# A fused state-space and expert kernel: TensorE signals the end of each matmul group by a drain

## The reference, cut to what matters

```python
x = x + _layernorm(_L0_attn_ref(_layernorm(x), ...))      # four state-space layers
x = x + _layernorm(_L0_ffn_ref(_layernorm(x), w1, w2, router_w))

# inside _L0_ffn_ref: x is 8192 tokens of 128 channels, 8 experts, 2 per token
probs = softmax(x @ router_w.T)
topk_weights, selected_experts = top_k(probs, 2)
for e in range(8):
    ew = sum(topk_weights * (selected_experts == e), axis=-1, keepdims=True)
    h = x @ w1[e].T                          # 128 -> 512
    y = (h[:, 256:] * silu(h[:, :256])) @ w2[e].T        # 256 -> 128
    out = out + y * ew
```

## Time and profile before

| what | value |
|---|---|
| median of 2 runs | 1078.75 us (1078.02 to 1079.48) |
| the profiled execution, its own time | 1082.16 us |
| its span (first to last instruction) | 1080.4 us |
| TensorE matmuls busy | 750.3 us, 69% of the span |
| VectorE busy | 779.1 us, 72% |
| ScalarE busy | 553.7 us, 51% |
| GpSimd busy | 478.7 us, 44% |

### The profile page before, as it was taken

One profiled execution on the slowest core, in us unless ns is written; L12 is line 12 of the kernel. 1 busy time (PEld: TensorE's weight loads), 2 busy tenths in 40 slices (PEclk: granted clock), 3 DMA queues, 4 the chain that ended last, 5 costly groups with the idle time before them and its releaser, 6 DMA issues.

```text
span 1080.4 us, 25428 instructions
## 1 busy us (share of the span) xinstructions
PE 750.3 (69%) x8885; PEld 637.1 (59%) x8886; DVE 779.1 (72%) x1919; ACT 553.7 (51%) x1130; POOL 478.7 (44%) x672
## 2 busy tenths in 40 slices
PE   0039357694878947695878876585878999999800
PEld 0028257573876747574876655464767877788700
DVE  8977876588575966588675998634455655699987
ACT  7627941179103951079103887434445656556545
POOL 2113323256442654257342776645566645655300
PEclk9999779898998979898888985578999999999955
DMA  7606699972999269981995002222334443211002
GB/s 283 268 1 205 192 386 386 344 258 92 355 353 374 93 231 387 341 308 43 363 387 239 1 11 78 76 81 91 116 122 134 138 132 116 77 35 35 23 39 117
DMA packets 114369, 197.50 MB, mean 183 GB/s; under 512 B 17372, under 2 KB 38376, under 8 KB 113512
## 3 DMA queue, kind: packets, MB, share of 16 engines
q1 hardware_dynamic: 107624, 182.62, 47.8%
q0 software_dynamic: 6656, 13.64, 4.0%
HBM read 164.38 MB, written 31.85 MB: 182 GB/s over the span
## 4 chain that ended last, share of the span: by engine, by line
PE 28%; issue 26%; POOL 18%; DVE 14%; ACT 7%; another core or an unknown queue 4%; DMA 2%; POOLq 1%; SPq 0%; ACTq 0%; DVEq 0%
PE bank L1212 12%; POOL zbuf L635 6%; PE bank L1230 6%; POOL rstd_of L624 5%; PE bank L1062 3%; PE bank L1040 2%; POOL z_sorted L695 1%; POOL sums L615 1%; DMA toep<-kernels_dram 1%; DVE stats L1852 1%; PE bank L1184 1%; POOL mean_of L620 1%; POOL m L622 1%; ACT ln_tmp L910 1%
## 5 line engine op out<-in xcount | busy, mean ns | idle before, releaser
L1062 PE MATMUL bank<-zbuf,toep 128*128 128x128 f16 (+3 forms) x3328 | 141.3, 203 | 95.5 <-DVE zbuf L1440 72.1
L1062 PEld LDWEIGHTS bank<-zbuf,toep 128*128 128x128 f16 x3328 | 137.9, 100 | 99.5 <-issue 48.6
L1212 PE MATMUL bank<-toep 128*128 128x256 f16 x1452 | 174.9, 276 | 11.3 <-issue 6.9
L1797 DVE TENSOR_TENSOR glu_work<-bank,glu_work 128x512 f32<-128x512 f32 x121 | 80.7, 689 | 118.9 <-issue 63.0
L1212 PEld LDWEIGHTS bank<-toep 128*128 (+1 forms) x1452 | 139.3, 99 | 35.4 <-issue 17.6
L635 POOL TENSOR_TENSOR zbuf<-zbuf,w_cur 128x256 f32<-128x256 f32 x120 | 90.0, 752 | 142.0 <-DVE zbuf L1504 142.0
L958 ACT ACTIVATE glu_work<-bank 128x512 f32<-128x512 f32 x121 | 68.9, 596 | 142.2 <-PE bank L1212 85.7
L695 POOL DMA_INDIRECT z_sorted<-toep x104 | 105.8, 1017 | 75.7 <-PE bank L1212 25.5
L1504 DVE TENSOR_REDUCE zbuf<-bank 128x256 f32<-128x512 f32 x128 | 87.1, 687 | 70.5 <-PE bank L1062 70.5
L1097 PE MATMUL bank<-wo_cur,glu_work 128*128 128x256 f32 x512 | 134.8, 408 | 2.5 <-ACT glu_work L855 2.2
L855 ACT ACTIVATE glu_work<-bank,unscale_cur 128x512 f32<-128x512 f32 x64 | 42.7, 668 | 165.0 <-PE bank L1084 164.7
(11 more groups left out here) (268 smaller groups left out, 1478.3 us busy)
## 6 DMA issues: line engine op xcount, KB each, us to landing
toep<-kernels_dram SPq DMA_DIRECT2D x104, 1024.0 KB, 13.9
glu_work<-kernels_dram SPq DMA_DIRECT2D x16, 1024.0 KB, 14.0
toep<-z_sorted SPq DMA_DIRECT2D x73, 128.0 KB
y_sorted<-toep SPq DMA_DIRECT2D x73, 128.0 KB
toep_last<-kernels_dram SPq DMA_DIRECT2D x8, 1024.0 KB, 14.1
z_sorted<-ln_tmp SPq DMA_DIRECT2D x2, 3584.0 KB, 26.2
hres<-in_x SPq DMA_DIRECT2D x1, 4096.0 KB, 12.9
toep<-in_x SPq DMA_DIRECT2D x1, 4096.0 KB, 21.8
```

The source lines that it names most:

```text
L1062: last = MM(dst[:, d * (B // 4):, :], toep_slot(g)[:, c, d * P:(d + 1) * P, k], z_conv[:, 0:QUADS - d * (B // 4), g * GROUP + c].rearrange ...
L1212: last = MM(out[:, piece % 2 * XP:(piece % 2 + 1) * XP], w1_row[:, pw, weights_at(s, piece * P, P)], xT_s[:, px * XP:(px + 1) * XP], start ...
L1797: TT(inner[:, s.at % 2, :], bank[3 + s.at % 2 * 2][:, :], gate_act[:, s.at % 2, :], ALU.mult).then_inc(s_inner, 1)
```

## The change

In the three helpers of the expert loop the increment no longer rides on the last matmul of the group. A drain instruction of TensorE is put behind the group, and the drain carries the increment. What is computed, the order of all else, all waits and all other engines' code are as before. There is one drain for each group, 315 in an execution.

```diff
@@ transpose_in
-                last.then_inc(s_xT, 1)
+                pe.drain().then_inc(s_xT, 1)
@@ first_product
-                last.then_inc(s_hid, 1)
+                pe.drain().then_inc(s_hid, 1)
@@ second_product
-                last.then_inc(s_yps, 1)
+                pe.drain().then_inc(s_yps, 1)
```

## The result

The changed kernel takes 1255.44 us (1251.55 to 1259.33) against 1078.75 us, a ratio of 1.1645 with an interval of 1.160 to 1.169. The forecast was 1275 us. The profiled span is 1257.6 us against 1080.4. All but 1 us of that lies in the expert loop: from its first matmul to the end of its last the loop takes 502.5 us instead of 326.3, which is 176.2 us more.

What follows compares the result with a forecast made beforehand. TensorE was taken to bound the dense and nearly the later sorted steps. To 1078.75 us came 124 us of drain costs (1203) and 72 us of drains held by GpSimd's bursts, giving 1275 us, range 1165 to 1390.

Steps and rivals of the forecast that it cites:

- The bound and the direction: Expert loop: TensorE bounds dense and nearly later sorted steps; slower by more than 22 us at 0.95.
- The rival on the other side: Locked cycles: drains signal past late completions, silu comes 2 to 3 us earlier, at most 18 us gained; same or faster 0.05.
- The price in dense steps: Dense cycles: each drain adds 0.33 us, from emptying the queue, the drain itself and restarting.
- Emptying: Behind each group: 0.16 us of the last matmul, formerly overlapped by the next group, is laid bare.
- The drain's own 0.05: Behind each group: the drain waits for the matmuls before it and itself adds about 0.05 us.
- The restart's 0.12: After each drain: restarting costs 0.12 us, taken from a dense cycle that waits at its start, 1.46 against 1.34 us.
- The price in sorted steps: Sorted cycles: drains, bare register instructions, slow starts and register loads add 3.4 us per cycle, bounds 2.0 and 4.5.
- The hold: Beside GpSimd's indirect DMA bursts: drains wait for late completions until the flush, 72 us more; 1275 us in all, chance 0.35.
- The sign named for the hold: Drains of over 1 us beside GpSimd's issues would show it; at most 0.3 us throughout would refute it.
- the matmuls in flight: Named way to be wrong: the delay beside bursts goes with the number of matmuls in flight; no size given.
- The clock: Rival, sorted cycles: TensorE falls to 1.2 GHz, 53 us on top for a third of them, 1328 us; chance 0.28.
- the 1203 forecast for drains that aren't held: Rival, expert loop: drains escape the wait beside GpSimd's bursts, so the sum of 1203 us stands; chance 0.25.

Runs made afterwards that it cites:

- the bare drains: Against the changed kernel, increments back on each group's last matmul, a drain without increment behind: 1202.78 us (ratio 1.1585) on one chip, 1264.58 us (1.1703) on another.

## Why the prediction was right, and which terms weren't

**The bound and the direction** hold: TensorE's stream was the bound, and no other engine covered the gaps. The rival on the other side, a signal that gets past the late completions, did not come: drains are held too.

**The price in dense steps**, 0.33 us a drain, was 0.245 us. Emptying was right at 0.16 us. The drain's own 0.05 was 0.02 us. The restart's 0.12 was 0.06 us; the row it was taken from the earlier trace rows held a passed wait besides. Behind the first product it is 0.33 us over the former distance, where such a wait does follow.

**The price in sorted steps**, 3.4 us a cycle, was about right. The single distances over the former ones add up to 0.245 (between transposes), 0.62 (to the second product), 0.46 and 0.49 (behind its halves, without a hold), 0.48 (between the wide ones) and 0.6 (to the transposes, the turns included), 2.9 us; the slow start of the two narrow groups, 0.78 us instead of 0.61 from first to last start, adds 0.3 us where I had 0.5.

**The hold** was the mis-sized term: 72 us forecast. Against the bare drains on the chip without it, the distances behind narrow groups cost 21.7 us more in sorted cycles (56.6 against 34.9), and those from the second narrow to the first wide group 11 us more in dense ones (19.8 against 8.7), 33 us together; the lateness of the held drains adds up to 34. The step that failed is that the sequencer "stands at the first or second drain inside a burst until the flush". Of 315 drains 256 weren't held at all, and all but one of the others stood for 1.3 us at most, not for the rest of a burst of 4 or 5 us; only the first second product's stood as forecast, 3.7 us. The sign named for the hold, drains of over 1 us, could not tell either: on the chip without a hold 80 of the bare drains last as long, since a drain's record holds its wait for the group. That the hold might go with the matmuls in flight was named as what would make me wrong. It would fit, since a drain has only its own group of at most twelve before it, but so had the drain of 3.7 us, and no run varies their number. How the hold comes about stays open.

**The clock** was a rival at 0.28 and was not in the sum; it came in part. In the sorted cycles the clock was granted at 1.2 GHz for 121 us, where it had been 26. Of 70 wide groups 12 ran wholly at that level (2.32 us from first to last start, against 1.21) and 18 partly (0.6 us more each), and of 66 narrow ones 23 (1.16 against 0.78 us). That is 34 us, against about 8 in the kernel before: 26 us. Hold and clock are not independent of each other: the drained loop is 51 us longer here than that of the bare drains on the chip without a hold, and 15 of these lie inside the groups, with 121 us at the lower level against 80. No run was made to hold the clock up, so this 26 us is an estimate from groups at either level and not from an experiment.

The sum, then: 176 us are 33 of the hold, 26 of the clock and, as what is left, 117 of emptied queues and bare sequencer work, for which I had 124. The 117 is a remainder and was not measured by itself. The forecast of 196 was near because a hold twice too large stood for a clock left out, and that is luck.

The 33 us are not what the change would cost less without a hold. On the chip without it the drains still cost 166 us, only 10 less: the drained kernel is 52 us faster there, and the kernel before is 42 us faster too. That the bare drains' 1202.78 us equals the 1203 forecast for drains that aren't held is a coincidence as well: it is 1036.69 + 166 and not 1078.75 + 124.

The Trainium skill (PSUM — Partial Sum Buffer, Engine vs sequencer instructions) has the increment belong on the matmul itself and a drain wait for the engine to go fully idle. It gives this as a matter of correctness. The runs agree on the second with the 0.02 us between the last matmul's end and the drain's, and add a price for taking the drain instead: 0.42 to 0.54 us per group here.

## What to carry to other kernels

Put the increment on the last matmul of a group. A drain in its place cost 0.25 us wherever the next group was ready to go, and 0.5 to 0.6 us where the sequencer had register arithmetic to do between groups, as in a loop with computed addresses. The drained loop also had its clock at 1.2 GHz for 121 us of its sorted cycles, where it had been 26. A wait of TensorE for its own signal cost nearly the same (1.135 against 1.1645), so let other engines do the waiting, and let TensorE's queue stay filled.

## What was unexpected of the hardware

In both traces of the kernel before TensorE's completions, as silu sees them, come late while GpSimd issues indirect DMAs: 86 of 121 signals, by up to 3.6 us, with TensorE itself stopped for 1.2 us in the earlier trace rows. On one chip none was late: with the drains on the transposes or on the second product alone, whose first products signal as before, 121 of 121 signals came within 0.02 us beside the same bursts, and the kernel before was 4% faster there (1036.69 us, known by its time alone). The kernels without gathers in the loop show that the lateness goes with the indirect DMAs on a chip that has the effect. What decides it stays open. All executions on that one chip were made on one occasion, so even that it is a lasting property of the chip isn't shown. A comparison across chips would have taken it for an effect of the code: 1202.78 us for the bare drains beside 1255.44 us for the change.
